# Full products of constants ahead of the last stage's small ones, and two norms behind a row of maxima

## The chip, the cores and the metric

The kernel runs on one core of one Trainium2 chip. The time is the device time of one execution in microseconds, the median of several runs. The profile is of one more execution, taken by the hardware profiler.

## The reference

The input is 8 batches of 256 rows of 256 numbers, with 120 context rows for each batch. Three attention layers and two feed-forward layers follow one another, each added to its input:

```python
x = x + cross_attention_0(layernorm(x), ctx, ctx, tau, delta)      # 16 heads of 16
x = x + block_1(layernorm(x))       # self-attention, then a choice of 1 of 8 experts for each row
x = x + cross_attention_2(layernorm(x), ctx, ctx, tau, delta)
x = x + routed_ffn(x)                                              # below

grouped  = x.reshape(2, 64, 32, 256)                               # groups of 32 rows
logits   = einsum('bntd,des->bntes', grouped, Wc) + bc + tie       # 32 experts, 4 sets
perm     = (logits == max over t of logits)                        # one row of each group for each (e, s)
permuted = einsum('bntd,bntes->bnesd', grouped, perm)
inner    = relu(einsum('bnesd,esdf->bnesf', permuted, W1) + b1)    # 256 -> 32
result   = einsum('bnesf,esdf->bnesd', inner, W2) + b2             # 32 -> 256
out      = einsum('bnesd,bntes->bntd', result, perm)
```

In the code x is normalized inside the last block too (`na`, `nb` with index 3 prepare a copy `Yz` of x for it).

## The kernel before, in words

The whole program is one list of steps, `STEPS`, and every engine walks through that list and issues what it has to do for each step, in that order. A step is a short name with its indices: `("na", 4, 0)` is the statistics of the first norm of batch 4. Batches are numbered through the layers: 0 to 7 are layer one (cross-attention), 8 to 15 layer two (self-attention and experts), 16 to 23 layer three (cross-attention, and the start of the last block). Waits between engines are semaphores; `Gate` leaves out waits that have already been passed.

The list for the attention layers is made by `pipeline`. It goes through the batches' score units in order, and after each unit (eight to a batch in the cross layers) it puts in the side work that is due by then. The due times are in units of a batch, relative to batch m; `T_CROSS` holds those of the norm and the queries of batch m: statistics (`na`), application (`nb`), the turn of the normed rows (`zt`), query projection (`qp`), split of the queries into three parts (`qs`, its low part on POOL), and their sends (`qd`, on SP's DMA queue). Batches 2 and 3 of a layer have times of their own. Tasks that are due in one pass come out in the order of their first time.

The row of maxima of a batch is eight products `mx` (TensorE, L796), each reduced by DVE (L1339), then `mh` (DVE splits the maxima into two parts, a cast L1348 and a difference L1350), then `mt` (TensorE turns them, L806). After `mt` the maxima are sent as a row of the queries (L1838), and the scores `sc` (L819) of that batch need them. `na` is three kinds of DVE instructions (L1291, L1294, L1296) and a power on POOL (L1632); `nb` is two DVE instructions (L1316); `zt` is L734. `p0`, `ps`, `p1`, `p2` finish the attention of a batch (reciprocal L1355 on DVE, five small operations L1656 to L1664 on POOL, L850, L861 on TensorE). `bg` is a gather of two indirect DMAs that POOL issues (L1688).

The last stage has an order written out by hand, `last_order`. `gp` is a sort: two times 12 products that pick rows by the permutation, each of 32 rows of the array (L991); the second dozen waits for the first. Its result is one of the two double banks `PS`, which ACT (L1217) and DVE (L1568) copy into `G` (`gc`). There are 16 sorts, two for each batch b. `e1` is the products of the first weights, four groups of 64 products with 32 columns of the array each (`sets_up`, L1007, two rows of the trace for each product). DVE and ACT add and clip. `e2` is the products of the second weights in eight groups, 32 rows of the array each (`sets_down`, L1029). Their banks are PS for the even groups and U and the three MB for the odd ones; DVE (L1584), ACT (L1229) and POOL (L1708) carry them to `R`. Turns (L1042) and the last products (L1053) follow.

TensorE is kept busy in some idle places already: steps `wm` (`keep_busy`, L1069) issue full products of constants, 128 rows by 256 columns, into PS.

Of the kernel before, what the change touches and what calls it, by code (L numbers as in the profile page):

```python
# [28 lines left out]
        (16, 2): (-1.75, -1.2), (17, 2): (0.05, 0.75), (18, 2): (0.75, 1.75)}  # L29
T_CROSS_2 = ((-2.45, -2.3, -1.5, -0.96, 0.03, 0.1), (), (-2.75, -2.45, -1.5, -0.96, 0.03, 0.1))  # L30
T_CROSS_3 = (-1.2, -1.1, 0.05, 0.25, 0.5, 0.75)
T_CROSS = (-3.7, -3.4, -2.95, -2.75, -2.5, -2.25)
T_SELF = (-3.95, -3.63, -3.61, -3.13, -2.78, -2.58, -2.33, -2.15)
EARLY = ((0, 0.213, 2.0), (0, 0.213, 0.9), (0, 0.35, 0.95))
# [30 lines left out]
def layer(n):  # L65
    return n // NB


def cross(n):
    return layer(n) != 1  # L70


def units(n):
    return 4 if cross(n) else 8
# [9 lines left out]
def pipeline(first, count, others):  # L84


    def even(pieces, lo, hi):
        return [lo + (hi - lo) * i / pieces for i in range(pieces)]

    def parted(what, n):  # L90
        return [(what + "h", n)] if (what, n) in PARTED else []

    tasks = []

    def task(times, *segments):
        tasks.append([times, list(segments), 0])

    for n in range(first, first + count):
        m, L = n - first, layer(n)
        e = EARLY[L][m] if m < 3 else m  # L100

        def at(times):
            return [(e if times[0] < -2 else m) + t for t in times]

        if cross(n):
            if n % 2 == 0 and n not in EARLY_KEYS.values():
                task(T_KEYS_2 if n == 2 else at(T_KEYS[L]), [("kp", n)] + parted("k", n), [("ks", n)],
                     [("kd", n), ("kr", n)])
            task([T_VALUES[L] if m < 4 else at(T_KEYS[L][1:])[0]], [("vp", n)])
            task(T_CROSS_2[L] if m == 2 else T_CROSS_3 if m == 3 else at(T_CROSS), [("na", n, 0)], [("nb", n, 0)], [("zt", n)],  # L110
                 [("qp", n)] + parted("q", n), [("qs", n)], [("qd", n)])
        else:
            task(at(T_SELF), [("na", n, 0)], [("nb", n, 1)], [("nb", n, 0)], [("zt", n)], [("qp", n)],
                 [("qs", n), ("kp", n)], [("qd", n), ("ks", n)], [("kr", n), ("kd", n), ("vp", n)])
        per = 4 if cross(n) else 8
        segments = []
        for qt in range(2):
            for u in range(per):
                segments.append(([("mh", n, 0)] if qt and u == 0 else []) + [("mx", n, qt * per + u)])
        segments += [[("mh", n, 1)], [("mt", n)]]  # L120
        if (n, L) in NEAR:
            task(even(2 * per + 3, *NEAR[n, L]), *segments)
        else:
            task(at(even(2 * per + 3, *T_MAX[L])), *segments)
        task(at(T_PROJECT_LAST if n == 15 else T_PROJECT[L]), [("p0", n)], [("ps", n)], [("p1", n)], [("p2", n)])
        if L == 1:
            task(at(T_AFTER_LAST if n == 14 else T_AFTER), [("xy", n), ("na", n, 2)], [("nb", n, 2), ("hs", n)], [("gt", n)], [("gl", n)], [("gr", n)],
                 [("gs", n)])
        if L == 2:
            task(at(T_FRONT), [("na", n, 3)], [("nb", n, 3)], [("ft", n)], [("fw", n)], [("fm", n)], [("fp", n)])  # L130
    for times, segments in others:
        task(times, *segments)
    tasks.sort(key=lambda t: t[0][0])
    out = []

    def sides(now):
        for t in tasks:
            times, segments, done = t
            while done < len(segments) and now >= times[min(done, len(times) - 1)]:
                out.extend(segments[done])  # L140
                done += 1
            t[2] = done

    for k in range(-60, 0):
        sides(k / 10)
    for n in range(first, first + count):
        m, U = n - first, units(n)
        for h in range(2 * U):
            if h % 2 == 0:
                out.append(("sc", n, h // 2))  # L150
            elif cross(n) and h > 1 or h % 4 == 1 and h > 1:

                out.append(("pv", n, h // 2 - 1))
            elif h == 1 and m and not cross(n - 1):
                out.append(("pv", n - 1, units(n - 1) - 1))
            sides(m + (h + 1) / (2 * U))
        if cross(n) or n + 1 == first + count:
            out.append(("pv", n, U - 1))
    for k in range(48):
        sides(count + k / 8)  # L160
    for t in tasks:
        for s in t[1][t[2]:]:
            out.extend(s)
    return out
# [34 lines left out]
def downs(engine, g):  # L199

    return sum(down_on(i, j) == engine for i in range(g + 1) for j in range(4))
# [134 lines left out]
BANKS = Ring(3, bank_users())  # L336
# [97 lines left out]
def build(nc, D, out, stack):  # L434
# [8 lines left out]
    def at(name, shape, dt, off):  # L443
        return nc.alloc_sbuf_tensor_at(name, shape, dt, offset=off)
# [29 lines left out]
    idb = g0.new("idb", [128, 128], BF)  # L474
    vec = g0.new("vec", [128, 160])
    cst = g0.new("cst", [128, 176])
    lo = g0.new("lo", [128, 2, 128], BF)
# [111 lines left out]
    zt = ma.ring("zt", 3, [128, 256])  # L589
# [59 lines left out]
    def bank(*step):  # L649
        return MB[BANKS.of[step]]  # L650

    def pair(*step):
        return PS[PAIRS.of[step]]
# [70 lines left out]
    def tensor(e):  # L724
        g = Gate(e, sems)
# [240 lines left out]
        def perm_turn(n):  # L966
# [4 lines left out]
                i = e.transpose(b[:, 128 * tt:128 * tt + 128], perm[:, 8 * p + 4 * tt:8 * p + 4 * tt + 4, :], idf[:, :])  # L971
            i.then_inc(sems["pt"], 1)

        def sort(b, k):
            ps, done = pair("gp", b, k), 4 * (count("gp", b, k) - 1)
            g.wait_ge("perm_turned", b + 1)
            g.wait_ge("f_turned", 2 * (b + 1))
            g.wait_ge("fz", b + 1)
            g.wait_ge("fl", b + 1)
            for signal in PAIRS.free["gp", b, k] or ():  # L980
                g.free(signal)

            for pair_of in ((0, 2), (1, 3)):
                if pair_of[0]:
                    g.wait_ge("gp", done + 2)
                for tt in range(2):
                    t = 2 * b + tt
                    for part in range(3):
                        z = z2[:, t, :] if part == 2 else z01[:, t, part, :]
                        for r in pair_of:  # L990
                            i = e.matmul(ps[:, 512 * (r // 2) + 256 * (r % 2) + 128 * tt:][:, 0:128],  # L991
                                         z[32 * r:32 * r + 32, 128 * k:128 * k + 128], pT[32 * r:32 * r + 32, t, :],
                                         start=part == 0, stop=part == 2)
                            if (tt, part) == (1, 2):
                                i.then_inc(sems["gp"], 1)

        def sets_up(b):
            m = bank("e1", b)
            g.wait_ge("d_v1", 16)
            g.wait_ge("sorted_a", copies("a", 7, 1))  # L1000
            g.wait_ge("sorted_b", copies("b", 7, 1))
            g.free(BANKS.free["e1", b])
            for q in range(8):
                for j in range(4):
                    s = 16 * (2 * b + q // 4) + 4 * j + q % 4
                    for k in range(2):
                        i = e.matmul(m[32 * j:32 * j + 32, 64 * q:64 * q + 64], v1[:, k, s, :], G[:, k, s, :],  # L1007
                                     start=k == 0, stop=k == 1)
            i.then_inc(sems["e1"], 1)

        def sets_down(n):
            b, half = GROUPS[n] // 2, GROUPS[n] % 2
            banks = [set_bank(n, j) for j in range(4)]
            g.wait_ge(f"d_v2{(0, 1, 2, 0)[b]}", 32 if b in (0, 3) else 16)
            g.wait_ge("relu", b + 1)
            if n == 0:
                g.wait_ge("sorted_a", copies("a", 7, 1))
                g.wait_ge("sorted_b", copies("b", 7, 1))
            elif n == 1:
                g.wait_ge("up", 4)  # L1020
                g.wait_ge("u_copied", 48)
            else:
                g.wait_ge("down", downs("b", n - 2))
                g.wait_ge("down_a", downs("a", n - 2))

            for q in range(4):
                for k in range(2):
                    for j in range(4):
                        i = e.matmul(banks[j][:, 128 * q + 64 * k:128 * q + 64 * k + 64],  # L1029
                                     v2[32 * j:32 * j + 32, 4 * GROUPS[n] + q, 128 * k:128 * k + 128],  # L1030
                                     Tmp[b][32 * j:32 * j + 32, 4 * half + q, :], start=True, stop=True)
                        if (q, k) == (3, 1):
                            i.then_inc(sems["e2"], 1)
# [1017 lines left out]
```

## Time and profile before

| | |
|---|---|
| time, median of 3 runs | 826.19 us (825.3 to 828.41) |
| the profiled execution's own time | 823.46 us |
| its span, from the first to the last instruction | 821.5 us |
| mean granted clock of TensorE | 0.956 |
| TensorE busy | 715.4 us (87%) |
| DVE, ACT, POOL busy | 57%, 44%, 31% |
| share of the chain that ended last | PE 52%, DVE 18%, ACT 8%, DMA 5%, POOL 5% |

The span is the profiled execution's; its time is 1.96 us more than the span. The granted clock is a share of 2.4 GHz: 1.00 is 2.4 GHz and 0.50 is 1.2 GHz. A busy share is an average over stages that are limited by different things.

### The profile page before, as it was taken

What the parts mean: (1) busy time and instruction counts of PE and PEld (TensorE: products, weight loads), DVE (VectorE), ACT (ScalarE), POOL (GpSimd) and SP (SyncE); (2) the same over time, 40 slices, a digit from 0 to 9 for tenths busy, and PEclk for the clock granted to TensorE, in tenths of its full rate; (3) what the DMA queues carried; (4) which work ended last, traced back from release to release, by engine and by line L of the source; (5) the groups of instructions that cost most, each with busy time, mean ns of one, the idle gap of its engine ahead of it and who ended that gap; (6) DMA issues with size and microseconds to landing.
All of it is one profiled execution on the core that took longest, in us unless ns stands there. A gap on an engine that the chain in (4) does not pass through costs nothing.

```text
span 821.5 us, 17575 instructions
## 1 busy us (share of the span) xinstructions
PE 715.4 (87%) x6672; PEld 547.8 (67%) x6672; DVE 469.9 (57%) x1206; ACT 363.3 (44%) x671; POOL 251.6 (31%) x320
## 2 busy tenths in 40 slices
PE   8777988889988999887999999989887887888898
PEld 6544655556666666577988899977655565555775
DVE  4757777777788798571221221224557677746375
ACT  4355656445656655602232322210454546545233
POOL 6722434323443321212120210005433434332140
PEclk9988999999999999999999999999979899977899
DMA  9697666755654584339647476502658363043302
GB/s 192 100 208 133 109 89 93 94 93 94 86 84 78 82 184 148 143 129 325 229 115 244 120 239 192 182 20 69 103 93 121 54 91 54 29 169 162 106 16 90
DMA packets 60534, 101.90 MB, mean 124 GB/s; under 512 B 7278, under 2 KB 50734, under 8 KB 55440
## 3 DMA queue, kind: packets, MB, share of 16 engines
q1 hardware_dynamic: 58020, 95.29, 51.1%
q0 software_dynamic: 1872, 5.11, 3.1%
q8 instruction: 54, 0.88, 0.5%
q10 hardware_dynamic: 560, 0.38, 0.2%
q14 instruction: 28, 0.23, 0.1%
HBM read 55.22 MB, written 7.21 MB: 76 GB/s over the span
## 4 chain that ended last, share of the span: by engine, by line
PE 52%; DVE 18%; ACT 8%; DMA 5%; issue 5%; POOL 5%; another core or an unknown queue 3%; SPq 3%; ACTq 0%; POOLq 0%; DVEq 0%
PE MB L754 8%; PE PS L934 8%; PE U L945 7%; DVE nma L1339 5%; PE MB L861 5%; PE U L837 4%; PE MB L796 3%; PE MB L777 3%; DMA mw<-in_mw 2%; PE PS L819 2%; SPq L1820 2%; PE MB L1042 2%; PE PS L991 2%; DVE nmb L1339 1%
## 5 line engine op out<-in xcount | busy, mean ns | idle before, releaser
L1339 DVE TENSOR_REDUCE nma<-MB 128x2 f32<-128x512 f32 (+1 forms) x192 | 122.2, 671 | 38.5 <-PE MB L796 38.5
L1157 ACT ACTIVATE Pa<-PS 128x1024 f32<-128x1024 f32 (+1 forms) x96 | 97.8, 1025 | 32.9 <-PE PS L819 31.5
L934 PE MATMUL PS<-mzT,mw 128*128 128x128 f32 x736 | 86.3, 276 | 3.9 <-DMA mw<-in_mw 3.9
L945 PE MATMUL U<-mw,mdT 128*128 x368 | 85.3, 386 | 4.6 <-DVE mdT L1531 2.3
L796 PE MATMUL MB<-QKa 99*128 99x120 bf16 (+1 forms) x512 | 70.9, 250 | 19.2 <-DVE nma L1339 4.9
L934 PEld LDWEIGHTS PS<-mzT,mw 128*128 128x128 f32 x736 | 84.1, 192 | 5.0 <-DMA mw<-in_mw 4.9
L1539 DVE TENSOR_TENSOR yt<-U,mb 128x256 f32<-128x256 f32 x23 | 9.8, 424 | 131.7 <-PE U L945 131.7
L945 PEld LDWEIGHTS U<-mw,mdT 128*128 128x128 f32 x368 | 69.4, 194 | 14.3 <-issue 5.6
L796 PEld LDWEIGHTS MB<-QKa 99*128 99x128 bf16 x512 | 37.7, 100 | 50.8 <-DVE nma L1339 13.5
L1632 POOL TENSOR_TENSOR mv<-mv,vec 128x2 f32<-128x2 f32 (+1 forms) x40 | 30.6, 765 | 113.9 <-DVE mv L1296 62.0
L819 PE MATMUL PS<-QKa 101*128 101x256 bf16 (+1 forms) x384 | 58.8, 277 | 2.1 <-DMA QKa<-mTa 2.1
L837 PE MATMUL U<-Pa,Vaa 128*32 128x256 f32 (+1 forms) x768 | 56.9, 399 | 2.0 <-ACT Pa L1157 2.0
L1179 ACT ACTIVATE mzT<-MB,vec 128x128 f32<-128x128 f32 x46 | 18.6, 456 | 88.7 <-PE MB L918 88.7
L1676 POOL DMA_INDIRECT zt<-hb,rows_of x23 | 22.0, 956 | 109.7 <-PE MB L918 97.8
L754 PE MATMUL MB<-zTa,W 128*128 128x256 f32 x192 | 48.3, 396 | 6.6 <-ACT zTa L1095 3.5
L1641 POOL TENSOR_TENSOR rqa<-tqa,spa 128x512 f32<-128x512 f32 (+1 forms) x28 | 32.4, 1158 | 69.0 <-ACT tqa L1136 46.4
L1339 DVE TENSOR_REDUCE nmb<-MB 128x4 f32<-128x480 f32 x64 | 39.8, 645 | 18.0 <-PE MB L796 17.3
L819 PEld LDWEIGHTS PS<-QKa 101*128 101x128 bf16 (+1 forms) x384 | 38.5, 112 | 9.9 <-issue 3.5
L754 PEld LDWEIGHTS MB<-zTa,W 128*128 128x128 f32 x192 | 35.3, 194 | 14.3 <-ACT zTa L1095 4.3
L1648 POOL TENSOR_TENSOR spa<-rqa,spa 128x512 bf16<-128x512 f32 (+1 forms) x28 | 32.6, 1163 | 33.2 <-ACT spa L1144 33.0
L1157 ACT ACTIVATE Pb<-PS 120x1024 f32<-120x1024 f32 x32 | 32.8, 1026 | 14.0 <-PE PS L819 13.8
L1189 ACT ACTIVATE mdT<-PS,vec 128x128 f32<-128x128 f32 x92 | 26.4, 372 | 28.4 <-PE PS L934 28.0
(227 smaller groups left out, 1388.3 us busy)
## 6 DMA issues: line engine op xcount, KB each, us to landing
mw<-in_mw SPq DMA_DIRECT2D x31, 1024.0 KB, 6.5
QKa<-spa SPq DMA_DIRECT2D x144, 128.0 KB, 4.8
Qb<-spb SPq DMA_DIRECT2D x48, 128.0 KB, 4.3
Oa<-Uba SPq DMA_DIRECT2D x16, 256.0 KB, 2.6
v<-in_v SPq DMA_DIRECT2D x1, 4096.0 KB, 13.4
v<-in_v SPq DMA_DIRECT2D x4, 1024.0 KB, 10.6
yb<-yt SPq DMA_DIRECT2D x23, 128.0 KB, 1.7
QKa<-spa SPq DMA_DIRECT2D x24, 120.0 KB, 4.0
```

The source lines that it names most:

```text
L754: i = e.matmul(b[:, 256 * half:256 * half + cols], w[:, k, 128 * half:128 * half + 128], rhs[:, k, :], start=k == 0, stop=k == 1)
L796: i = e.matmul(b[:, keys * j:keys * j + keys], Q[0:99, h0 + j, 128 * qt:128 * qt + 128], K[0:99, h0 + j, 0:keys], start=True, stop=True)
L819: i = e.matmul(ps[0:keys, c:c + 256], K[0:101, h, keys * kt:keys * kt + keys], Q[0:101, h, :], start=True, stop=True)
L837: i = e.matmul(U[32 * j:32 * j + 32, 256 * gg:256 * gg + 256], V[0:keys, kt, 8 * half + 4 * gg + j, :], p[0:keys, c:c + 256], start=kt == ...
L861: e.matmul(b[:, 256 * tt:256 * tt + 256], o[:, half, 128 * tt:128 * tt + 128], W.o[:, half, :], start=half == 0, stop=False)
L934: i = e.matmul(ps[:, 128 * f:128 * f + 128], w[:, k, 128 * f:128 * f + 128], zz[:, k, :], start=k == 0, stop=k == 1)
L945: i = e.matmul(U[:, 0:256], mdT[j % 2][:, f, :], w2[:, bass.ds(expert[j], 1), f, :], start=f == 0, stop=f == 7)
L1157: e.activation(p[0:keys, :], ps[0:keys, :], ACT.Exp, scale=0.25).then_inc(sems["exp"], 1)
L1339: e.tensor_reduce(A.nm[qt][:, h0:h0 + heads], b[:, 0:heads * keys].rearrange("p (h s) -> p h s", h=heads), AX.X, ALU.max, negate=True).the ...
L1632: e.tensor_tensor(rs[r][:, 0:w], ve[r][:, 0:w], mhalf[:, 0:w], ALU.pow).then_inc(sems["rs"], 1)
L1641: e.tensor_tensor(r, f32, hi, ALU.subtract).then_inc(sems["split_r"], 1)
L1648: e.tensor_tensor(low, whole(what, n)[1], mid_, ALU.subtract).then_inc(sems["split_l"], 1)
```

## The change

The due times of `na` and `nb` of the fifth and sixth batch of the two cross layers (4, 5, 20, 21) become 0.4 and 0.3 of a batch later; the later times of that task stay. A new function `keep_clock` issues n full products of constants (the identity by `lo`, 128 rows by 256 columns) into a bank that the step is about to write anyway. It is called in every sort after its waits (3 products for b of 0 and 1, else 2), ahead of the first `e1` group (8 products, before the waits for the weights and the copies), and in every `e2` group after its waits (2 products). The wait for the bank of `e1` moves ahead of its other waits.

```diff
+T_CROSS_45 = (-3.3, -3.1, -2.95, -2.75, -2.5, -2.25)
 T_CROSS = (-3.7, -3.4, -2.95, -2.75, -2.5, -2.25)
...
-            task(T_CROSS_2[L] if m == 2 else T_CROSS_3 if m == 3 else at(T_CROSS), [("na", n, 0)], [("nb", n, 0)], [("zt", n)],
+            task(T_CROSS_2[L] if m == 2 else T_CROSS_3 if m == 3 else at(T_CROSS_45 if m in (4, 5) else T_CROSS), [("na", n, 0)], [("nb", n, 0)], [("zt", n)],
                  [("qp", n)] + parted("q", n), [("qs", n)], [("qd", n)])
...
+        def keep_clock(bank, n):
+
+            g.wait_ge("idb", 1)
+            g.wait_ge("d_lo", 16)
+            for _ in range(n):
+                e.matmul(bank[:, 0:256], idb[:, :], lo[:, :, :].rearrange("p a n -> p (a n)"), start=True, stop=True)
+
         def sort(b, k):
...
             for signal in PAIRS.free["gp", b, k] or ():
                 g.free(signal)
+            keep_clock(ps, 3 if b < 2 else 2)
...
         def sets_up(b):
             m = bank("e1", b)
+            g.free(BANKS.free["e1", b])
+            if b == 0:
+                keep_clock(m, 8)
             g.wait_ge("d_v1", 16)
             g.wait_ge("sorted_a", copies("a", 7, 1))
             g.wait_ge("sorted_b", copies("b", 7, 1))
-            g.free(BANKS.free["e1", b])
...
                 g.wait_ge("down", downs("b", n - 2))
                 g.wait_ge("down_a", downs("a", n - 2))
+            keep_clock(banks[0], 2)
```

## Rows read from the trace of the kernel before

**Rows 1.** Engines' busy time by stretch, granted clock (PEclk) after POOL.

```profile
core 0: us, PE busy (x) PEld busy (x) DVE busy (x) ACT busy (x) POOL busy (x), PEclk, DMA share, GB/s
66.90:73.70 6.80, 5.62 (x46) 2.92 (x46) 5.75 (x14) 2.31 (x4) 3.53 (x7) 0.50 0.78 124
626.70:630.10 3.40, 3.40 (x32) 2.03 (x25) 2.73 (x7) 1.62 (x2) 0.61 (x2) 0.50 0.38 92
...
732.50:739.30 6.80, 6.71 (x44) 4.76 (x37) 3.27 (x9) 3.34 (x6) 1.15 (x1) 0.50 0.89 386
739.30:749.50 10.20, 7.94 (x138) 5.29 (x137) 8.78 (x21) 5.75 (x11) 4.28 (x4) 1.00 0.77 323
749.50:761.10 11.60, 10.04 (x170) 7.01 (x170) 5.52 (x8) 5.38 (x8) 0.00 (x0) 0.50 0.01 3
761.10:766.60 5.50, 5.43 (x205) 5.46 (x209) 0.69 (x1) 0.63 (x1) 0.00 (x0) 0.50 0.01 3
...
774.10:792.60 18.50, 16.69 (x522) 15.70 (x520) 13.84 (x22) 6.87 (x12) 11.34 (x11) 1.00 0.21 71
```

**Rows 2.** TensorE's timeline, 726 to 752 us: projection and sorts (start, length, line).

```profile
726.86 1.13 PE L861 MATMUL MB<-W,Ob 128*128 128x256 f32 x4 [0.28 <-DVE Ob L1378]
...
735.30 2.07 PE L861 MATMUL MB<-W,Ob 128*128 128x256 f32 x4
...
740.28 1.86 PE L991 MATMUL PS<-pT,z 32*128 32x128 bf16 x48
...
746.24 1.11 PE L991 MATMUL PS<-pT,z 32*128 32x128 bf16 x24
...
751.72 8.39 PE L991 MATMUL PS<-pT,z 32*128 32x128 bf16 x144
```

**Rows 3.** TensorE's timeline where full products of constants (L1069) stand.

```profile
29.68 1.04 PE L1069 MATMUL PS<-y 128*128 128x256 bf16 x8
...
790.35 0.28 PE L1029 MATMUL MB<-etmp,v 32*128 32x64 f32 x3
790.57 0.61 PE L1069 MATMUL PS<-lo,idb 128*128 128x256 bf16 x4
```

**Rows 4.** TensorE's timeline of all four L1007 groups.

```profile
761.17 7.49 PE L1007 MATMUL MB<-G,v 128*32 128x64 f32 x331 [1.06 <-ACT G L1217]
...
769.37 2.04 PE L1007 MATMUL MB<-G,v 128*32 128x64 f32 x128 [0.71 <-issue]
...
773.10 1.08 PE L1007 MATMUL MB<-G,v 128*32 128x64 f32 x53 [1.69 <-issue]
```

**Rows 5.** The chain that ended last, in L1029's stage: first and last of four.

```profile
778.62 1.90 DVE R L1584 x3
...
790.72 1.88 DVE R L1584 x3
```

**Rows 6.** Timeline around the turn of batch 18's maxima (L806).

```profile
619.48 0.38 PE L796 MATMUL MB<-Kb,Qb 99*128 99x120 bf16 x4 [1.38 <-DMA Qb<-spb]
...
621.12 0.74 DVE L1291 BATCH_NORM_STATS2 st<-x 128x6 f32<-128x256 f32 x2
...
622.19 0.93 DVE L1355 RECIPROCAL Lb<-Lb 32x128 f32<-32x128 f32 x1
...
623.60 0.73 POOL L1632 TENSOR_TENSOR mv<-mv,vec 128x2 f32<-128x2 f32 x1
...
623.67 1.83 DVE L1348 CAST Mhb<-nmb 128x16 bf16<-128x16 f32 x1
...
624.33 1.14 POOL L1648 TENSOR_TENSOR spb<-rqb,spb 128x512 bf16<-128x512 f32 x1
...
625.79 0.28 PE L806 MATMUL MB<-idb,Mhb 128*32 128x128 bf16 x2 [3.74 <-DVE Mhb L1350]
```

**Rows 7.** Timeline around the turn of batch 2's maxima (L806).

```profile
67.64 0.17 DVE L1348 CAST Mha<-nma 128x16 bf16<-128x16 f32 x1
...
68.08 0.40 PE L806 MATMUL MB<-idb,Mha 128*32 128x128 bf16 x2 [1.92 <-DVE Mha L1350]
```

**Rows 8.** TensorE's timeline at the first product of batch 2's maxima (L796).

```profile
49.06 0.56 PE L796 MATMUL MB<-QKa 99*128 99x120 bf16 x4 [0.43 <-issue]
```

## The prediction

> **What bounds the kernel now.** No engine is full over the whole span, so I read stage by stage, and looked only where the change touches. The table of stretches comes first [rows 1]: from 732.5 to 792.6 us, the routed feed-forward at the end, TensorE is the busiest engine in each stretch but 739.3 to 749.5, and the granted clock is at its lower level (0.50, which is 1.2 GHz) in three of them: 732.5 to 739.3, 749.5 to 761.1 and 761.1 to 766.6, together 23.9 us. The reader should see that in two of these TensorE is busy nearly all the time, so it isn't idleness alone that goes with the lower level: from 749.5 on nearly all its instructions are the sorts' products of 32 rows, while the clock stayed up in 739.3 to 749.5, where sorts stand between products of the full array. It rose again only inside the 128-row products of L1007.
>
> Then TensorE's own timeline and its rows by stage [rows 2 to 5], for what the higher clock would give and what a full product costs. Last, the two rows of maxima behind which norms move: DVE's, TensorE's and POOL's timelines [rows 6 to 8]. There the row to see is TensorE's turn of the maxima (L806), which sat idle 3.74 us at 625.79 and 1.92 us at 68.08, each time until DVE's split of the maxima was done; a norm's statistics stand on DVE just ahead.
>
> **The change, part by part. First, the norms.** A segment comes out at the first eighth of a batch at which its time is due. For the fifth batch the statistics (na) move from 0.375 to 0.75 and the application (nb) from 0.625 to 1.0; the sixth a batch later. So na now follows the second (third) batch's last maxima, their split (mh) and turn (mt), on DVE and on POOL, whose power also moves behind the low split of the queries (qs) before it. nb still precedes zt in the planner's order, and zt keeps its time, though in two sixth batches it now falls behind p1 (layer one) or p2 (layer three) in TensorE's queue. No instruction is added or removed.
>
> *Batch 21.* Its statistics hold DVE from 621.12 to 622.19, before the reciprocal; then comes the last maxima, then a cast of 1.83 us that starts at 623.67, and TensorE goes on at 625.79 [rows 6]. Without the statistics the cast starts 1.07 us sooner. The cast's length is more than the statistics': the same cast took 0.17 us at other times, as at 67.64 [rows 7]; here it ended with POOL's low split of 1.14 us, which followed the moved power of 0.73 us from 623.60 [rows 6]. About 622.6 POOL would still be issuing its two gathers, so I expect the short cast: 1.07 + 1.66 = 2.7 us off the wait. The Trainium skill, "SBUF — State Buffer", section "Who interferes with whom", says that a cast of VectorE and an instruction of GpSimd may exclude each other on a shared port pair; the trace agrees (1.83 against 0.17 us), and if the low split got there first, the cast would be as long as before.
>
> What is late next: p1 waits for POOL's five small operations behind the low split, and these only gain the 0.73 us of the power. Before, TensorE reached p1 only after work at the lower clock that lasted until 630.1 [rows 1], so there is room for most of the 2.7 us. *Batch 20.* TensorE waited 1.38 us at 619.48 for batch 19's queries [rows 6]; batch 20's power stands in POOL's queue ahead of a gather and of those queries' low split, and waits there for DVE. With it gone the wait should go too, but most of it is taken up by the chain after it (ACT's splits and the gathers). Layer three in sum: 2.6 us; bounds 0.4 (only the first turn) and 4.6 (all waits and half of a stretch at the upper clock).
>
> *Batches 4 and 5.* At 68.08 the wait was 1.92 us and the cast short (0.17) [rows 7]; the same three operations of statistics cost the same 1.07 us ahead of it, and POOL and SP behind it have the order of batch 21 without gathers: 1.07, less what TensorE then does a little longer at the lower clock (0.50 in 66.9 to 73.7 [rows 1]): 0.8; bounds 0 and 1.6. For batch 4 the same turn would come earlier too, but the product after it started only at 49.06, after 0.43 us that no instruction in the trace ended [rows 8]; I take that for the landing of its queries, which the change doesn't touch: 0.3; bounds 0 and 1.1. Norms together: **−3.7 us** (−0.4 to −7.3).
>
> **Second, the full products.** At the full clock eight of 128×256 take 1.04 us and four 0.61 [rows 3], so 0.11 each behind another. All sixty (12 + 24 in the sorts, 8 ahead of the first L1007 group, 16 in the groups of L1029) stand behind the waits for their bank, so what hides them must be idle time after those.
>
> *Sorts, price.* Two sorts back to back took 1.86 us and a lone one 1.11, because a sort's first half runs beside the second half of the one before [rows 2]. A full product uses all rows and ends that. The step from L1029's last row to a full one took 0.22 us [rows 3], about the tail already inside the 1.11. So a sort with two products is 1.11 + 0.22 + 0.04 = 1.37 us, against 8.39 / 6 = 1.40 at the lower clock. The Trainium skill, "TensorEngine Tiling (Array Packing)", section "Key Properties", says that a change of tiling mode drains TensorE, which speaks against this change; without the drain a sort would be 0.93 + 0.22 = 1.15 us and the six would give 1.3 us more. The rows bear out the drain, so the sum goes by 1.37.
>
> *732.5 to 739.3.* At the upper clock the projection's four products take 1.13 instead of 2.07 us, twice, and the smaller ones about 0.6 less: −2.5. Four sorts with three products each ahead of it: +1.1, part of it under ACT's copies. So −1.4; if this stretch's clock is not held, or would have held anyway, +1.1. *739.3 to 749.5.* Here the last batch's norm goes round DVE, POOL and ACT and TensorE is busy 7.94 of 10.2 us [rows 1]; of five sorts' products some 0.4 us is left on the path: +0.4 (0 to 1.5). *749.5 to 761.1.* Six sorts 6 × 0.03 and the sort and turn before them 0.6: −0.8; +5 if the clock stays down (two products 0.44, the broken overlap 0.25, seven times). *L1007.* The eight products fit in the idle 1.06 us before it [rows 4], the wait for the last copies. At the upper clock 128 rows take 2.04 us; all 512 then 8.16, and with the two idle stretches "issue" of 0.71 and 1.69 us, 10.56 against 13.01 from 761.17 to 774.18: −2.4. Those stretches came only when the rows ran at the upper clock, so the two faster groups may get one too (0.71 each at the least seen): I take −1.7; bounds −2.4 and +1.0 (two of 1.69). *L1029.* The clock is 1.00 there already [rows 1], so this can only cost. The chain alternates a group with three additions of DVE (1.90 us), two groups in (790.72 − 778.62) / 3 = 4.03 us [rows 5]. Two products with both transitions add about 0.47 between groups where 0.1 to 0.3 was idle: two groups become 4.5, four times 0.5: +2.0; bounds +0.5 and +2.8. Products together: −1.4 + 0.4 − 0.8 − 1.7 + 2.0 = **−1.5 us**.
>
> **Sum.** −5.2 us on the profiled execution's 823.46 (a span of 821.5 and 1.96 around it) gives 818.3; that execution is 2.7 us under the median of the runs, 826.19, and by the ratio 0.9937 the median becomes **821.0 us**. Half a per cent, 4.1 us, is about what a measurement can tell from no change, so faster means under 822.1, slower over 830.3.
>
> **Rivals.** *The products give back what they win*: the sorts and L1007 don't speed up beyond their own cost, because the drain and the waits for issue take it, and the norms alone pay. For it: 1.37 against 1.40 us; against: L1007's rows at 2.04 us a group. Products 0 to +1.5, norms −3.7: 822.5 to 824. *The norms don't reach the end*: TensorE comes earlier but meets the same landings, p1's POOL operations and zt behind p1 and p2. For it: the start at 49.06 [rows 8]; against: at 625.79 nothing but DVE was waited for [rows 6]. Norms −1, products −1.5: about 823.5. *The clock isn't held, and it is slower*: the place is the six sorts from 749.5; if the clock goes down while sorts with two products run, these take 2.1 us, the sparse stretch gets longer and sparser, and stays down until L1007. +5 there, +1.5 before, +2 in L1029, L1007 unchanged, norms −3.7: 831. It decides at whether two full products a sort are enough; the trace shows full clock with sorts and other full products mixed, and the lower with sorts alone, nothing between. *No effect*: norms and products both within a microsecond, 825 to 827.
>
> **Chances.** My forecast as it stands, 817 to 822: 0.50. Products give back: 0.17. Norms don't reach the end: 0.12. Not held: 0.10. No effect: 0.06; a stronger gain (both upper bounds), 814 to 817: 0.05. Faster takes the forecast, the strong gain and a little of two rivals: 0.57; slower, most of the not-held case and a little more: 0.10; same 0.33. Range 815 to 827.5, from the stronger gain to no effect; the not-held case is left out.
>
> **What would show it.** In the changed profile: clock 1.00 from about 727 to the first L1007 row; six sorts of the last batches at about 1.37 us each; L1007 from first to last row 10.5 to 11.5 us with "issue" ahead of more groups; two L1029 groups in 4.5 us; L806's idle time at batch 18 near 1 us and batch 2's near 0.9; no DMA wait of 1.4 us before batch 19's maxima. Wrong would be: 0.50 in the sorts, a cast still of 1.8 us, or an unchanged 4.03 us in L1029.

## The result: slower, and the profile after

The median went from 825.75 us (823.75 to 828.41, 4 runs) to 845.19 us (840.21 to 848.65, 4 runs): ratio 1.023, 95% interval 1.016 to 1.030. All four executions lie above all four of before. The profiled one takes 848.65 us, its span is 845.7 us, and the mean granted clock is 0.939 where it was 0.956. Medians here are of all executions of a kernel; ratios leave out those over 1.5% above their kernel's fastest.

In the changed code the lines of the last stage are about twelve further down: the sorts (L991) are L1001, `e1` (L1007) is L1019, `e2` (L1029) is L1042, the turn of the maxima (L806) is L808, and the new products are L981. The engines' busy time by stretch, which answers to [rows 1]:

```profile
core 0: us, PE busy (x) PEld busy (x) DVE busy (x) ACT busy (x) POOL busy (x), PEclk, DMA share, GB/s
726.30:740.00 13.70, 12.54 (x188) 8.49 (x187) 10.40 (x29) 7.03 (x14) 3.71 (x4) 1.00 0.85 340
740.00:749.50 9.50, 9.23 (x88) 5.97 (x86) 4.49 (x10) 3.81 (x7) 2.31 (x2) 0.50 0.53 218
749.50:765.40 15.90, 15.28 (x186) 9.13 (x184) 5.06 (x7) 5.37 (x8) 0.00 (x0) 0.50 0.01 1
...
767.20:779.60 12.40, 9.57 (x514) 9.10 (x514) 2.08 (x3) 1.90 (x3) 0.00 (x0) 0.86 0.21 65
779.60:784.30 4.70, 2.73 (x69) 2.31 (x68) 0.70 (x2) 0.73 (x2) 0.00 (x0) 1.00 0.80 289
784.30:813.80 29.50, 29.50 (x466) 25.71 (x466) 11.76 (x19) 5.95 (x11) 10.30 (x10) 0.50 0.01 2
```

The reader should look at the last line first. `e2`, which ran wholly at 1.00 before [rows 1], spends 29.5 us at 0.50. The first sorts did hold the clock (1.00 up to 740), the later ones did not. TensorE's timeline of the same stage answers to [rows 2, 4]:

```profile
763.23 0.61 PE L981 MATMUL PS<-lo,idb 128*128 128x256 bf16 x2
763.76 1.73 PE L1001 MATMUL PS<-pT,z 32*128 32x128 bf16 x24
765.43 1.89 PE L981 MATMUL MB<-lo,idb 128*128 128x256 bf16 x8
767.24 5.92 PE L1019 MATMUL MB<-G,v 128*32 128x64 f32 x288
774.59 2.05 PE L1019 MATMUL MB<-G,v 128*32 128x64 f32 x128 [1.43 <-issue]
778.04 1.60 PE L1019 MATMUL MB<-G,v 128*32 128x64 f32 x96 [1.41 <-issue]
779.58 0.39 PE L981 MATMUL PS<-lo,idb 128*128 128x256 bf16 x2
779.90 1.11 PE L1042 MATMUL PS<-etmp,v 32*128 32x64 f32 x30
782.99 1.32 PE L1042 MATMUL PS<-etmp,v 32*128 32x64 f32 x34 [1.97 <-issue]
...
788.89 3.69 PE L1042 MATMUL PS<-etmp,v 32*128 32x64 f32 x64
...
797.21 3.69 PE L1042 MATMUL PS<-etmp,v 32*128 32x64 f32 x64
```

The last sorts take 2.20 us each (763.23 to 765.43). TensorE waits for "issue" as it did before, but at other places; that is idle time that no instruction and no DMA of the program ended. Before, the waits came after 331 and 459 of `e1`'s 512 rows [rows 4], and a short third one in `e2`'s second group, about 76 rows in (TensorE's timeline of the kernel before):

```profile
776.92 0.33 PE L1029 MATMUL MB<-etmp,v 32*128 32x64 f32 x3 [0.37 <-issue]
```

Now they come after 288 and 416, and the third, of 1.97 us, stands in the middle of `e2`'s first group. Right behind it the clock is at 0.50, and two `e2` groups take 8.3 us (788.89 to 797.21) instead of 4.03 [rows 5].

So the time can be followed by first rows. At 730 us the changed kernel is 2.6 us ahead (the same rows of DVE and ACT in both traces, median of their differences); `e1` begins 6.1 us late (767.24 against 761.17), `e2` 5.8 us late (779.90 against 774.11), the span ends 24.1 us late. The sorts lost 8.7 us, `e1` nothing, `e2` and what follows it 18.3 us.

The norms did as forecast at both turns. TensorE's and DVE's timelines there answer to [rows 6, 7]:

```profile
66.53 0.17 DVE L1361 CAST Mha<-nma 128x16 bf16<-128x16 f32 x1
...
66.97 0.29 PE L808 MATMUL MB<-idb,Mha 128*32 128x128 bf16 x2 [0.72 <-DVE Mha L1363]
...
625.55 0.18 DVE L1361 CAST Mhb<-nmb 128x16 bf16<-128x16 f32 x1
...
625.99 0.28 PE L808 MATMUL MB<-idb,Mhb 128*32 128x128 bf16 x2 [0.99 <-DVE Mhb L1363]
```

### The profile page after: what moved, and what is told of

Same layout as the page of the kernel before. It is cut to its first block, busy times and chain, and to the rows that moved or that the text cites. A ratio compares the mean times of both kernels' runs of the same rounds, so it can differ in the third digit from the quotient of the medians.

```text
span 845.7 us, 17693 instructions
## 1 busy us (share of the span) xinstructions
PE 742.1 (88%) x6732; PEld 565.3 (67%) x6732; DVE 467.1 (55%) x1206; ACT 364.7 (43%) x671; POOL 252.2 (30%) x320
## 4 chain that ended last, share of the span: by engine, by line
PE 57%; DVE 16%; ACT 7%; DMA 6%; issue 6%; POOL 5%; SPq 3%; ACTq 0%; DVEq 0%; POOLq 0%
PE U L947 9%; PE PS L936 8%; PE MB L756 8%; DVE nma L1352 4%; PE MB L863 4%; PE U L839 3%; PE MB L779 3%; PE MB L798 2%; PE PS L1001 2%; PE PS L821 2%; PE MB L1055 2%; PE PS L1082 2%; SPq L1833 2%; PE PS L1042 2%; PE U L1042 2%
## 5 line engine op out<-in xcount | busy, mean ns | idle before, releaser
L947 PE MATMUL U<-mw,mdT 128*128 x368 | 83.6, 380 | 5.0 <-DVE mdT L1544 2.3
L1552 DVE TENSOR_TENSOR yt<-U,mb 128x256 f32<-128x256 f32 x23 | 9.8, 425 | 129.0 <-PE U L947 129.0
L947 PEld LDWEIGHTS U<-mw,mdT 128*128 128x128 f32 x368 | 68.1, 190 | 14.2 <-issue 5.9
L821 PE MATMUL PS<-QKa 101*128 101x256 bf16 (+1 forms) x384 | 59.6, 280 | 5.0 <-DMA QKa<-mTa 5.0
L1082 PE MATMUL PS<-lo,idb 128*128 128x256 bf16 x318 | 39.5, 276 | 1.2 <-issue 1.1
## 6 DMA issues: line engine op xcount, KB each, us to landing
v<-in_v SPq DMA_DIRECT2D x1, 4096.0 KB, 13.5
v<-in_v SPq DMA_DIRECT2D x4, 1024.0 KB, 10.4
```

The costliest lines, as they stand in the source:

```text
L821: i = e.matmul(ps[0:keys, c:c + 256], K[0:101, h, keys * kt:keys * kt + keys], Q[0:101, h, :], start=True, stop=True)
L947: i = e.matmul(U[:, 0:256], mdT[j % 2][:, f, :], w2[:, bass.ds(expert[j], 1), f, :], start=f == 0, stop=f == 7)
L1082: e.matmul(PS[0][:, 0:256], a, b, start=True, stop=True)
```

## The experiments

Three theories. Theory 1: the products in `e2` bring its clock down. Theory 2: the norms cost layer one more than they give. Theory 3, formed after the first four runs: the instruction count decides. A wait for "issue" comes after each 128 rows of `e1` and `e2`; the 44 products ahead of `e1` (12 + 24 in the sorts, 8 ahead of the first group) put these waits 44 rows earlier, one of them into `e2`'s first group, and there it costs the clock.

### One part at a time

**Norms only.** All `keep_clock` calls are out.

> Only the later due times of the norms; no product of constants is added (the e1 bank is still waited for ahead of the other waits). Theory 1 (the loss is all in the last stage's products): the norms keep the 2.65 us that the changed kernel was ahead at 730 us, and the last stage is as before: 822 to 824. Theory 2 (the norms hurt layer one for good: the changed kernel was 6.9 us behind from 165 us to the end of layer two, and made up for it later by other luck): layer one 4 to 7 us behind again, time 826 to 831. Rival (what the layers win or lose is the clock's, at other places in each execution): the offset at 165 us is neither -3 nor +7, and the time is within 1 us of before.

829.07 us (816.03 to 832.54) where before was 833.14 (820.15 to 839.09) on that chip. The times lie in two groups, 816.03 and 819.47, and four of 828.74 to 832.54, and settle neither theory. The profiled execution is 4.2 us behind at 165 us, as Theory 2 expects, but 4.8 us ahead at 730 us; its span is 4.2 us shorter than that of before, and `e2` is at 1.00.

**Products only.**

```diff
-at(T_CROSS_45 if m in (4, 5) else T_CROSS)
+at(T_CROSS)
```

> All 60 products of constants, the norms as before. Theory 1: the granted clock is 0.50 in the sorts with two products and again in the L1042 (e2) groups; 5 us lost up to e1 and 14 to 17 us in e2: 844 to 849. Rival (the products fall to the lower clock only because the norms moved the stage, and at the old place they would hold it): 824 to 829.

845.42 us, ratio 1.022 (1.011 to 1.033): the whole loss. But not by Theory 1's path alone: here the sorts kept 1.00 until 755.1 us, and `e2` fell all the same, behind a wait of 1.67 us in its first group.

**No products in `e2`.** Only `keep_clock(banks[0], 2)` is out.

> The changed kernel without the two products ahead of each e2 group; sorts and the eight ahead of e1 stay. Theory 1 (the products inside e2 bring the clock down there and then cost twice): e2 is back at 1.00 and at 4.0 us for two groups, 16 us less than the changed kernel: 827 to 831. Rival (e2's clock falls for another reason, as the longer issue waits in e1 or the stage's late start): 0.50 stays in e2, 838 to 843.

843.2 us, ratio 1.017 (1.005 to 1.029). Theory 1 fails: without a product in it `e2` has the wait (2.02 us), and is at 0.50.

**Products in `e2` alone.**

> Only the two products ahead of each e2 group, added to the kernel before (norms as before, no products in the sorts or ahead of e1). Theory 1: e2 falls to 0.50 and takes 14 to 17 us more: 840 to 843. Rival A (the products cost only their own length and two drains each, the clock stays 1.00 unless it was already low ahead of e1): two groups 4.5 us, 827 to 829.

834.91 us where before was 833.14: ratio 1.001 (0.996 to 1.006). Its twelve executions fall apart into six of 822.6 to 831.6 and six of 838.2 to 845.4; the profiled one (839.07) has `e2` at 0.50. So the products by themselves don't cost the loss in every execution: half of the times are near Rival A's, half near Theory 1's.

### The count of instructions, and nothing else

**Before, with 44 pairs more.** A pair is a weight load and its product.

```diff
-            for _ in range(IDLE[step]):
-                e.matmul(PS[0][:, 0:256], a, b, start=True, stop=True)
+            n, c = (150, 181) if step == ("se", NTILE - 1) else (IDLE[step], 256)
+            for _ in range(n):
+                e.matmul(PS[0][:, 0:c], a, b[:, 0:c], start=True, stop=True)
```

> The kernel before, with 44 more instruction pairs and no more work: the 106 full products of constants ahead of layer three (27136 columns) become 150 of 181 columns (27150). Theory 3 (an 'issue' wait comes after each 128 or so products of e1 and e2, at a place that the count of instructions sets, and decides e2's clock): the waits move from e1's products 332 and 460 and e2's 76 to 288, 416 and 32, as in the changed kernel; in e2's first group TensorE waits near 2 us instead of 0.37, the clock falls to 0.50 there and stays, and the last stage takes 12 to 14 us longer: 836 to 842 if before is 826. Rival (the full products themselves bring the clock down in e2, by their changes of tiling or their time): e2 stays at 1.00, within 2 us of before.

842.86 us where before was 831.96: ratio 1.017 (1.011 to 1.023), all six executions at 835.47 or more. The last stage is the kernel before, untouched, and TensorE's timeline of it shows the waits of the changed kernel:

```profile
779.37 1.62 PE L1007 MATMUL MB<-G,v 128*32 128x64 f32 x97 [1.42 <-issue]
780.92 1.11 PE L1029 MATMUL PS<-etmp,v 32*128 32x64 f32 x31
784.01 1.80 PE L1029 MATMUL PS<-etmp,v 32*128 32x64 f32 x33 [1.99 <-issue]
...
788.82 3.82 PE L1029 MATMUL PS<-etmp,v 32*128 32x64 f32 x64
...
795.64 3.82 PE L1029 MATMUL PS<-etmp,v 32*128 32x64 f32 x64
```

The pad was not free: the stage begins 7.6 us late (`e1` at 768.77). But the span ends 20.5 us late; the other 12.9 us are lost behind that.

**The changed kernel, with 84 pairs more** (106 products become 190 of 143 columns), which makes 128 with the 44.

> The changed kernel, with 84 more instruction pairs and no more work ahead of layer three (106 products of 256 columns become 190 of 143), which with the 44 added products ahead of e1 makes 128, so that the waits for issue fall again at e1's products 332 and 460 and e2's 72. Theory 3: the wait in e2 is under 0.6 us, the clock stays at 1.00 through e2, 10 to 16 us faster than the changed kernel (829 to 835 where that takes 845), and two e2 groups take 4.5 us. Rival (the products bring it down): as the changed kernel, 0.50 in e2.

829.57 us where before was 831.96, ratio 1.001 (0.996 to 1.006), with a pad that again cost some 5 us. The engines' busy time by stretch shows the sorts, `e1` and `e2` all upheld:

```profile
733.00:761.50 28.50, 26.28 (x445) 17.34 (x445) 20.17 (x45) 16.02 (x28) 6.18 (x6) 1.00 0.56 228
763.92:776.90 12.98, 8.76 (x514) 8.17 (x514) 2.08 (x3) 1.89 (x3) 0.00 (x0) 0.96 0.20 64
776.90:795.00 18.10, 18.02 (x524) 15.72 (x524) 12.04 (x19) 6.27 (x11) 10.30 (x10) 1.00 0.22 77
```

and TensorE's timeline of it why that gives `e1` nothing:

```profile
768.97 2.05 PE L1019 MATMUL MB<-G,v 128*32 128x64 f32 x128 [1.41 <-issue]
772.43 2.05 PE L1019 MATMUL MB<-G,v 128*32 128x64 f32 x128 [1.41 <-issue]
775.88 1.05 PE L1019 MATMUL MB<-G,v 128*32 128x64 f32 x52 [1.41 <-issue]
```

At 1.00, 128 rows take 2.05 us and then wait 1.41: 3.46 in all. At 0.50, 205 rows took 5.50 us [rows 1], which is 3.43 for 128. `e1` is no faster at the upper level: 13.0 us here as before.

**84 pairs more in two other kernels**: one with layer three's norms alone, and the kernel before.

> No full products; the later norms in layer three alone (batches 20 and 21); 84 instruction pairs more ahead of layer three, which puts the wait for issue at e2's product 120, where the first two groups' slower products have given it time. Theory 3 with the norms read from the traces (layer three gains 4 us or so, layer one loses 3 by stretches at 0.50 that the kernel before has not): no wait in e2's first group, 1.00 in e2, 4 us under the next kernel. Rival (the norms' gain in layer three is the clock's chance): as the next kernel, within 1.5 us.

> The kernel before, with 84 more instruction pairs and no more work ahead of layer three. Theory 3: the wait for issue falls on e2's product 120 and is hidden, e2 is at 1.00 in all executions; where some executions of the kernel before run e2 at 0.50, this one is faster in the median by up to 5 us and no execution is over 830; it is never slower. Rival (the place of the waits doesn't matter): the same times as before, spread as widely.

829.22 us, ratio 1.001 (0.995 to 1.006), and 841.94 us (827.34 to 846.5), where before was 831.96. Both profiles have `e2` at 1.00 and end 4.4 and 6.0 us late; `e1` begins 4.6 and 6.3 us late in them. But four of the six executions of the second are at 840 or more, and five of the twelve of the first at 836 or more: "never slower" is a miss, and so is the 1.00 "in all executions", as far as times tell.

**A pad of small products.** The 106 products become 97 with 53 of 32 columns and 128×32 weights between them (for 84 pairs: 88 and 102).

> The kernel before with 44 more instruction pairs, as in the run with 150 products of 181 columns, but padded so that the pad itself should take no longer: 97 of the 106 products of constants stay and 53 small ones (32 by 32) stand between them. Theory 3: nothing changes up to 755 us (that pad was 7.6 us late there), the waits for issue are at e1's products 288 and 416 and e2's 32, near 2 us there, e2 at 0.50, 11 to 14 us slower than before. Rival (the earlier run was slow by its pad): within 3 us of before.

> The changed kernel with the waits for issue put back to e1's products 332 and 460 (84 instruction pairs more: 88 of the 106 products and 102 small ones between them). Theory 3: as the run with 190 products of 143 columns, without the 5 us that its pad was late: e2 at 1.00, two groups 4.8 us, 822 to 828 where before is 826 to 832, 15 to 20 us under the changed kernel. Rival (the place of the waits is only one of the causes; the two products a group or the sorts bring e2 down in most executions): 835 or more.

> Only the products in the sorts and the eight ahead of e1, none in e2, the norms as before, the waits for issue at their old places by the same pad. What the products are worth where they do no harm: sorts 1.37 us each at 1.00 against 1.40 at 0.50, and e1's 128 products paced by their instructions at 3.45 us at either clock. Theory 3: within 2 us of before (the products buy nothing even at 1.00). Rival (the higher clock pays once the wait is out of e2): 3 to 5 us faster.

847.0, 849.92 and 863.93 us where before was 829.87 (ratios 1.023, 1.026, 1.029). The pad was no better: it made layer three 7 us late in the first and 27 us in the others, so only the last stage can be read, in the table below. In it the first falls as the changed kernel did, and the second holds. The third, with its waits at their old places, falls too, which Theory 3 did not expect.

### The same place with nothing added

**44 pairs fewer instead of 84 more**: 30 of the 106 products stay, and 16 in four-byte numbers, each of two slower passes, stand among them (32 rows). The whole pad takes 10.4 us, where the 106 took 11.7.

```diff
-            for _ in range(IDLE[step]):
+            wide = 16 if step == ("se", NTILE - 1) else 0
+            if wide:
+                g.wait_ge("d_idf", 16)
+            for i in range(30 if wide else IDLE[step]):
                 e.matmul(PS[0][:, 0:256], a, b, start=True, stop=True)
+                if i < wide:
+                    e.matmul(PS[0][:, 0:256].rearrange("p (a n) -> p a n", a=2), idf[:, :], over(idf[:, :], 2, 1), start=True, stop=True)
```

In the changed kernel:

> The changed kernel, with 44 instruction pairs fewer ahead of layer three and about the same busy time there, so that the waits for issue fall at e1's products 332 and 460 and, in e2, after the first group. Theory 3 (the wait in e2's first group is what costs): e2 at 1.00, two groups 4.8 us, and the whole 14 to 18 us under the changed kernel: 826 to 832 where before is 826 to 832. Rival (the other parts cost as much): 838 or more.

821.18 us where before was 828.55: ratio 0.9952 (0.9915 to 0.9988). That is 24 us under the changed kernel, where 14 to 18 were expected, and a little faster than before. Its slowest execution was the profiled one (835.56 us), whose last sorts are at 0.50; its `e2` is at 1.00:

```profile
743.00:770.00 27.00, 26.10 (x280) 16.10 (x278) 10.34 (x18) 9.96 (x16) 2.31 (x2) 0.50 0.19 78
...
784.30:803.00 18.70, 18.70 (x536) 16.38 (x534) 12.45 (x20) 6.66 (x12) 10.29 (x10) 1.00 0.22 76
```

Then with parts of the change, and layer three's norms with and without the shift:

> The products in the sorts and ahead of e1 alone, none in e2, norms as before, the same 44 pairs fewer. Theory 3: e2 at 1.00 and the products worth nothing by themselves (a sort 1.37 us at 1.00 against 1.40 at 0.50, e1 paced at 3.45 us for 128 products at either clock), within 2.5 us of before. Rival (at the upper clock they pay): 3 to 5 us faster. Where the sorts lose the clock (2.20 us each) it is 5 us slower, and the profile says which of the two it was.

> All 60 products and the 44 pairs fewer, the norms as in the kernel before. If the products earn the gain, by keeping e2 at 1.00 in nearly all executions: 820 to 823 where before is 828.6. Rival (the norms earn it): 825 to 829, like the kernel with products in the sorts alone (825.7).

> All 60 products and the 44 pairs fewer, but the later norms in layer three alone. If the norms of layer one cost what the profiles say (2.8 us, through stretches at 0.50 that the kernel before has not), 2 to 4 us under the kernel with both layers' norms moved (821.2 where before was 828.6): 817 to 820. Rival (those stretches are chance): the same within 1.5 us.

> Only the later norms of batches 20 and 21 in layer three; no product, no pad, the norms of layer one as before. By the traces layer three gains 4 us and layer one loses 2.8 when its norms move too: here 4 us faster than before, and the offset against before is 0 to 2 us up to 600 us and 3 to 5 us less from 670 on. Rival (the gain in layer three is the clock's chance in three profiles): within 1 us of before.

> The later norms of layer three alone, with 44 pairs fewer, so that the wait for issue in e2 falls at its product 120, where the profile of a padded kernel shows none. Theory 3: 1 to 5 us faster than the same without this shift (822.5 where before was 829.9), as no execution loses e2. Rival (the executions of before differ by other stretches): the same as without the shift, within 2 us.

Sorts and `e1` alone: 825.7 us where before was 828.55, ratio 0.997 (0.993 to 1.002). All products: 827.33 where before was 829.69, ratio 0.999 (0.994 to 1.003), the rival's outcome, that the norms earn the gain. All products with layer three's norms: 823.05 there, ratio 0.990 (0.986 to 0.994), the best ratio of all, though single executions reach 845.69; under before it is no better than with both layers' norms, again the rival's outcome. Layer three's norms alone: 822.49 where before was 829.87, ratio 0.996 (0.992 to 1.001); but the profile has no such gain, 0.2 us ahead of before at 600 us and 0.3 at 700, where 3 to 5 us were expected from 670 on. With 44 pairs fewer they take 828.48 us where before was 828.55, ratio 1.003 (0.998 to 1.008), a miss: the profile has no wait in `e2`'s first group, and `e2` at 0.50, behind a wait of 1.66 us ahead of the last 8 rows of `e1`.

### All profiles side by side

From `e2`'s first product to the end of the span, by the row of `e2` (about) at which the count of instructions puts a wait for "issue":

| kernel | products in `e2` | the wait at | clock in `e2` | us to the end |
|---|---|---|---|---|
| before; norms only; norms of layer three | no | `e2`'s row 76 | 1.00 | 47.4; 47.5; 47.4 |
| sorts and `e1`, 44 fewer | no | row 76 | 1.00 | 47.4 |
| layer three, 84 more; before, 84 more | no | row 120 | 1.00 | 46.9; 47.1 |
| sorts and `e1`, small pad | no | row 76 | 0.50 | 56.6 |
| layer three, 44 fewer | no | row 120 | 0.50 | 57.3 |
| no products in `e2`; before, 44 more; the same, small pad | no | **row 32** | 0.50 | 59.6; 61.1; 60.6 |
| changed, 84 more; small pad; 44 fewer; all products, 44 fewer | yes | row 72 | 1.00 | 49.1; 49.4; 48.8; 49.4 |
| products in `e2` alone | yes | row 72 | 0.50 | 60.9 |
| all products with layer three's norms, 44 fewer | yes | row 72 | 0.50 | 64.9 |
| changed; products only | yes | **row 32** | 0.50 | 65.8; 65.4 |

That the count sets the place can be read from all 19 profiles: counted from the program's first product, the waits of 0.3 us and more in `e1` and `e2` come after product 5588, 5716, 5844, 5972 or 6100, within two, whichever stage has reached it.

With the wait at row 32 `e2` fell in five profiles of five, and none of the 28 executions of these five kernels was under 834 us. At the other places it held in ten of fourteen. Upheld, the sixteen products cost 1.4 to 2.0 us; fallen, `e2` costs 9 to 13.7 us more without and 13.5 to 18.3 with them. The waits move together, so that it is the one in `e2` and not those in `e1` that costs the clock is argued from where the clock falls, not shown.

## Why the prediction was wrong

**The step that failed** is the term for L1029: "The clock is 1.00 there already [rows 1], so this can only cost", +2.0 us with bounds of +0.5 and +2.8. The products there cost what it says, 1.4 to 2.0 us, where the clock holds. But it doesn't hold, and the cause is not in L1029. The prediction saw the waits for "issue" and counted one more of them for L1007; it did not ask what sets their place. That is the count of instructions ahead of them: the 44 products "behind the waits for their bank", costed by their own time, moved a wait from row 76 of `e2`, where 0.37 us of it were left, to row 32, where it was 1.97 us. 44 pairs without any of the change, ahead of layer three, do the same (1.99 us, 0.50, 12.9 us); 44 pairs taken away undo it (821.18 us). The undone kernel's ratio, 0.9952, is close to the one forecast, 821.0 / 826.19 = 0.9937, but partly by luck, as the terms below missed in both directions.

**The rival that came nearest**, "The clock isn't held, and it is slower", had the wrong place: its 831 us priced the sorts, and kept L1029 at 1.00. In this profile its sorts did come: 2.20 us each where it said 2.1, 8.7 us lost up to `e1`. But of the ten profiles with products in the sorts, six held the clock into the last sorts, at 1.36 each in the run with 84 pairs more, where the forecast was 1.37. So the price was right at both levels, and whether two products are enough differs from one profile to the next. That they win next to nothing even then (1.36 against 1.40) the prediction had said. The first sorts and the projection behind them did earn their term but for 0.2 us (−1.4): from 2.6 us ahead at 730 to 3.8 at 740, and 1.2 us in each of the other nine.

**L1007** was mis-sized, −1.7 forecast. First row to last it took 12.4 us (767.24 to 779.64) in the changed kernel against 13.0, 13.0 where it ran nearly all at 1.00, and up to 14.2 in the ten profiles with the eight products ahead of it: 128 rows and the wait behind them took 3.45 to 4.0 us at 1.00 and 3.43 at 0.50. So the term was −0.6 to +1.2, at worst just outside its bound of +1.0; faster products only turned into longer waits.

**The norms** were right in their mechanism at batch 18 (0.99 us of wait, near 1 forecast; the cast 0.18) and batch 2 (0.72, 0.9 forecast). Their sum over the layers is the same rows of DVE and ACT set against those of before, median of each stretch, in all profiles. From 590–605 to 690–710 us the ten profiles with moved norms of layer three win 4.8 us in the mean (0.1 to 7.0; 0.1 is the run with nothing else changed), the nine others, that of before among them, lose 0.3 (from 3.2 won to 1.7 lost): 5.1 us, where the term was 2.6 and its bound 4.6. At 250 us, behind layer one, the six with moved norms there are 4.2 us late, the thirteen others 1.4: layer one loses 2.8 us where −1.1 was forecast. In the changed kernel's profile these are stretches at 0.50 (125.6 to 129.0, 149.5 to 152.9) that the kernel before has not; all six have two such between 122 and 153 us, and of the thirteen others two have one. The times don't bear the loss out: with all products and 44 pairs fewer, the kernel with layer one's norms is 7.4 us under before, the one without 6.6.

**What stays open.** Why `e2` falls in four of fourteen profiles with the wait elsewhere, and in which executions of the kernel before: these ran from 818.07 us at a mean clock of 0.967 to 843.07 at 0.927. No run here controlled it. That the waits are for the fetch of instructions is read from times and counts; no run changed the fetch. They come after 128 weight loads and 128 products, and each of the 57 waits for "issue" of 0.3 us and more after 740 us, in 19 profiles, ended 1.2 to 1.6 us after a 16 KB packet of kind "instruction" had landed. From `e1`'s start to `e2`'s end the view of the DMA queues of the changed kernel (queue and kind: packets, MB, share of 16 engines) lists 8 such packets, 0.13 MB:

```profile
q1 hardware_dynamic: 288, 2.10, 13.3%
q8 instruction: 8, 0.13, 1.1%
```

The Trainium skill, "Trainium Architecture — The Big Picture", section "The software stack", gives an instruction 64 bytes; by that figure 16 KB are 256 instructions, an estimate, as many as stand between two waits. The same section tells of moving the streams when the program is loaded; the trace has such packets in the middle of the run.

## What to carry to other kernels

Where the profile shows waits for "issue" at even distances in an engine's rows, count the rows between them, and before adding instructions anywhere ahead, work out on which row the waits will fall: an added instruction costs its own time and a shift of all that follow. That a stage is at the upper clock before the change does not make it so after; the term has two values, and the sum should carry both. Before a change is judged by its time, run it once with the count of instructions put back: here that turned 1.023 into 0.995.

## What was not expected of the hardware

Small products between full ones cost far more than their columns. With one product of 128×32 weights and 32 columns behind each full one, full products came every 0.33 us (559.65 to 559.98 in the second run with the small pad, TensorE's timeline) instead of 0.11, the pace of the 106 of before (11.74 us):

```profile
559.65 0.27 PE L1083 MATMUL PS<-lo,idb 128*128 128x256 bf16 x1
559.86 0.19 PE L1085 MATMUL PS<-lo,idb 128*32 128x32 bf16 x1
559.98 0.28 PE L1083 MATMUL PS<-lo,idb 128*128 128x256 bf16 x1
```

And many short products in a row came to wait for "issue": in the run with 150 products of 181 columns, 110 of them took 8.78 us, 0.080 each, the next 11 came one to three at a time between waits for "issue" of 0.26 to 1.10 us, and the last 29 took 4.20 us, 0.145 each; layer three began 5 us late.
